# Second attention: values of four heads per group, a ring of eight heads' probabilities, value projections two slots later

## The chip, the cores and the metric

The kernel runs on one core of a Trainium2 chip. The metric is the device time of one execution in microseconds; lower is better. Most executions of a kernel agree within 0.3%.

## What is computed

Two transformer blocks on eight images of 16x16 tokens with 192 channels, in float32. The first block attends inside 14x14 windows (12 heads of 16 channels), the second over the whole image of 256 tokens (12 heads of 48 channels). Both add decomposed relative positions (a term by row and one by column) to the scores. Each attention is followed by an MLP of four times the width. The change is in the second block's attention:

```
xn = layernorm(x) * ln1_scale + ln1_offset          # per image: 256 tokens x 192
q = xn @ wq + bq;  k = xn @ wk + bk;  v = xn @ wv + bv   # 12 heads x 48
logits = q k^T / sqrt(48) + bias_h(q) + bias_w(q)   # per head: 256 x 256
attn = softmax(logits)
out = (attn @ v) @ wo + bo
x = x + out;  x = x + mlp(x)
```

## The kernel before

The program is written by hand for each engine's queue, with semaphores between them. It goes through four stages, each over the eight images: attention 0, MLP 0, attention 1, MLP 1 (classes `Attention0`, `Mlp`, `Attention1`; the base class `Attention` holds the common steps). All of x stays in the on-chip memory, as do the weights.

An image of attention 1 has 12 **slots**, one for each head (`run`, `step`; `pe_slot`, `act_slot` and `dve_slot` say what each engine does in slot u). The heads are software-pipelined: in slot u TensorE computes the scores of head u + 3 (L1239, two matmuls of 256 columns, 80 rows deep: 48 channels and 32 rows that carry the positions), then transposes the probabilities of head u into a PSUM bank (L1246, four transposes). ScalarE takes the exponentials of head u + 2 (L663), VectorE normalizes head u + 1 (L671, L674) and takes the maximum of head u + 3 (L653). The transposed probabilities are copied from PSUM into `PT1` (L693), by VectorE for every fourth head and by ScalarE for the others; `PT1` holds four heads, and the copy for head u waits until the values that read that place are done (`pt_free`).

The values of heads 2q and 2q + 1 are computed when both are copied: `pv_after` names the slot after which group q is complete, and `VALUES_BEHIND = 1` puts its matmuls (L1266, four of 256 columns: two key halves by two heads, each head on 64 columns of the array) into the next slot. So values stand in slots 2, 4, 6, 8, 10, and for the last pair in slot 0 of the next image. They fill 256 of the 512 columns of `O_BANK`; ScalarE copies them to `AO1` (L1274, `act_ao`) before the next pair may be written. In slot 1 the output projection follows (L1285, `pe_back`), in the same bank.

The next image's front is spread over the same slots (`pe_fronts`, `act_fronts`, `dve_fronts`). In slot 2 its normalized rows are transposed (L705) and scaled into `xnT`, a rounded `xnH`, and the low part of their difference (L1310, VectorE). Slots 3 to 5 compute its q and k (L1318, six matmuls for each half) from these, with evictions by ScalarE and VectorE; the first waits for the low part. At the end of slot 5 come 64 small matmuls for the position terms (L1378). In slot 6 ScalarE (L1397) and VectorE (L1405) copy these to `rel_dense`. Then SyncE and GpSimd each issue four transfers of 48 KB that spread them over the rows of the operand Q (L1436), behind the larger transfers of q and k (L1416, L1420). Slots 7 and 8 compute v for the two halves of the tokens (L1346, `pe_v`; 12 matmuls of 288 columns each). In slot 9 TensorE computes the first scores of the next image. They wait for all these transfers:

```
                if u == 0:
                    eng.wait_ge(self.scat, n.at(64, 64))
                    eng.wait_ge(self.relscat, n.at(64, 64))
                    eng.wait_ge(self.relscat_w, n.at(64, 64))
```

The front of the first image runs ahead of the stage without slots, and the last image has no follower, so seven images carry a front in their slots.

Of the kernel before, what the change touches and what calls it, by code (L numbers as in the profile page):

```python
# [39 lines left out]
P = 128  # L40
# [84 lines left out]
def build(nc, a, out):  # L125
    with ExitStack() as ctx:
# [117 lines left out]
        area = sb("area", [P, 2 * NT * HEADS * 64 + (8 + NPAIR) * T])  # L244
# [3 lines left out]
        PT1 = area[:, 3072:3072 + 8 * T].rearrange("p (b k q) -> p b k q", b=4, k=2)  # L248
        AO1 = area[:, 3072 + 8 * T:3072 + (8 + NPAIR) * T].rearrange("p (q t) -> p q t", q=NPAIR)
# [360 lines left out]
        class Attention:  # L610
# [76 lines left out]
            def pt_out(self, eng, n, u, copy):  # L687

                eng.wait_ge(self.t_rdy, n.at(self.NU, u + 1))
                per, k = self.pt_free(u)  # L690
                if n.counts(per, k):
                    eng.wait_ge(self.pv, n.at(per, k))
                copy(*self.pt_views(u)).then_inc(self.pt[self.pt_engine(u)], 1)  # L693
# [186 lines left out]
        class Attention0(Attention):  # L880
# [339 lines left out]
        class Attention1(Attention):  # L1220
            G_USES = (10, 10)
            G_OUTS = (11, 11)
            V_SLOT = 7
# [26 lines left out]
            def pt_views(self, u):  # L1250
# [19 lines left out]
            def act_ao(self, eng, n, q):  # L1270
                eng.wait_ge(self.pv, n.at(NPAIR, q + 1))
# [4 lines left out]
            def dve_ao(self, eng, n, q):  # L1276
                pass

            def pe_back(self, eng, n):
                eng.wait_ge(self.ao[0], n.at(NPAIR, NPAIR))  # L1280
# [74 lines left out]
            def act_v(self, eng, n, t):  # L1355
                eng.wait_ge(self.g_rdy[0], n.at(10, 9 + t))
                if n.counts(NPAIR, -NPAIR):
                    eng.wait_ge(self.pv, n.at(NPAIR, -NPAIR))
                nc.scalar.copy(*self.v_views(n, t, 0)).then_inc(self.g_out[0], 1)

            def dve_v(self, eng, n, t):
                eng.wait_ge(self.g_rdy[1], n.at(10, 9 + t))
                if n.counts(NPAIR, -NPAIR):
                    eng.wait_ge(self.pv, n.at(NPAIR, -NPAIR))
# [100 lines left out]
            def setup(self):  # L1465
# [6 lines left out]
                                  5: each(self.pe_qk, (5,)) + [self.pe_rel], 7: each(self.pe_v, (0,)),  # L1472
                                  8: each(self.pe_v, (1,))}
                self.act_fronts = {2: [self.act_xn], 3: each(self.act_q, (0, 1, 2)), 4: each(self.act_q, (3, 4)),
                                   5: each(self.act_q, (5,)), 6: [self.act_rel], 7: each(self.act_v, (0,)),
                                   8: each(self.act_v, (1,))}
                self.dve_fronts = {0: [self.dve_stats], 1: [self.dve_xhat], 2: [self.dve_xn], 3: each(self.dve_k, (0, 1, 2)),
                                   4: each(self.dve_k, (3, 4)), 5: each(self.dve_k, (5,)), 6: [self.dve_rel],
                                   7: each(self.dve_v, (0,)), 8: each(self.dve_v, (1,))}
# [4 lines left out]
                        {2 * q + 1: [q] for q in range(NPAIR)})  # L1484
# [289 lines left out]
```

## Time and profile before

| | |
|---|---|
| runs, us | 877.87, 874.0, 875.62 (median 875.62) |
| the profiled execution | 876.63 us, span 874.8 us |
| mean granted clock of TensorE | 0.967 |
| busy share of the span: TensorE / VectorE / ScalarE / GpSimd | 90% / 59% / 50% / 15% |
| attention 1 in the span | about 433 to 795 us |
| its scores / transposes / values, busy us | 108.1 / 59.8 / 53.3 |
| chain that ended last, by engine | TensorE 78%, VectorE 12%, issue 3%, ScalarE 3%, DMA 2% |

The span runs from the first to the last instruction; the execution's time has a little around it. A row of a timeline gives the start, the length, engine, line, operation, output and inputs with their shape, the count of merged instructions, and in brackets the idle time just before with what ended it.
### The profile page before, as it was taken

How to read it: one execution, taken by the hardware profiler on the slowest of the kernel's cores; microseconds unless marked ns; L12 is line 12 of the kernel's file. 1: busy time of each engine (PE TensorE's matmuls, PEld its weight loads, DVE VectorE, ACT ScalarE, POOL GpSimd, SP SyncE). 2: the span in 40 equal slices, each digit the busy share in tenths (PEclk: the TensorE clock that was granted, in tenths of full speed). 3: DMA queues.
4: the chain of work that ended last, by engine and by line, in shares of the span. 5: the costliest groups of instructions: out<-in, count | busy, mean ns of one | idle time of the engine just before them, and what ended most of it. 6: DMA issues, size and time to landing. Idle time of an engine off the chain costs nothing.

```text
span 874.8 us, 18893 instructions
## 1 busy us (share of the span) xinstructions
PE 787.8 (90%) x6794; PEld 641.5 (73%) x6794; DVE 518.5 (59%) x1518; ACT 434.4 (50%) x1421; POOL 127.7 (15%) x243
## 2 busy tenths in 40 slices
PE   3788989898898977789979999999999999997998
PEld 2566656575675744789967788888888888876998
DVE  6156777757667676454426565666666666674442
ACT  2045565645656554444335455555555555554432
POOL 7200110101111010142320101010101010101111
PEclk9989999989999997899987999999999999999999
DMA  7362101010110100100040404040404040400001
GB/s 144 73 147 36 20 17 25 11 33 10 29 20 17 29 8 1 37 1 1 1 73 0 73 2 73 1 74 1 73 1 74 1 75 1 74 1 1 19 22 34
DMA packets 38092, 29.23 MB, mean 33 GB/s; under 512 B 11926, under 2 KB 36274, under 8 KB 38000
## 3 DMA queue, kind: packets, MB, share of 16 engines
q1 hardware_dynamic: 34974, 25.71, 16.2%
q0 software_dynamic: 2048, 1.89, 1.2%
q8 instruction: 55, 0.90, 0.5%
q10 hardware_dynamic: 978, 0.43, 0.3%
q14 instruction: 37, 0.30, 0.1%
HBM read 7.94 MB, written 1.57 MB: 11 GB/s over the span
## 4 chain that ended last, share of the span: by engine, by line
PE 78%; DVE 12%; issue 3%; ACT 3%; DMA 2%; ACTq 1%; POOL 1%; SPq 1%; DVEq 0%; POOLq 0%
PE bank L1239 10%; PE bank L1318 8%; PE bank L475 7%; PE bank L496 7%; PE bank L1266 5%; PE bank L1246 5%; PE bank L1115 5%; PE bank L946 4%; PE bank L922 4%; PE bank L1285 4%; PE bank L1047 3%; PE bank L1378 3%; DVE Pb L674 2%; PE bank L973 2%; PE bank L1012 2%
## 5 line engine op out<-in xcount | busy, mean ns | idle before, releaser
L663 ACT ACTIVATE Pb<-bank,nmax 128x256 f32<-128x256 f32 (+1 forms) x432 | 191.9, 452 | 88.1 <-DVE nmax L653 85.7
L653 DVE TENSOR_REDUCE nmax<-bank 128x2 f32<-128x392 f32 (+2 forms) x240 | 138.8, 579 | 44.7 <-PE bank L1239 32.9
L674 DVE TENSOR_SCALAR Pb<-Pb,rsum 128x196 f32<-128x196 f32 (+2 forms) x432 | 133.7, 347 | 8.7 <-DVE rsum L671 0.2
L693 ACT COPY area<-bank 98x392 f32<-98x392 f32 (+1 forms) x144 | 77.3, 538 | 86.6 <-PE bank L1246 75.0
L1239 PE MATMUL bank<-QK 80*128 80x256 f32 x384 | 108.1, 407 | 8.1 <-DMA QK<-rel_dense 6.7
L1239 PEld LDWEIGHTS bank<-QK 80*128 80x128 f32 x384 | 69.7, 199 | 28.7 <-issue 16.2
L663 ACT ACTIVATION_READ_ACCUMULATOR Pb<-bank,nmax 128x1 f32 x432 | 87.4, 202 | 0.0
L946 PE MATMUL bank<-ident,Pb 128*98 128x128 f32 x384 | 64.0, 291 | 19.2 <-DVE Pb L674 19.1
L485 ACT ACTIVATE area<-bank,fc1b 128x256 f32<-128x256 f32 x96 | 45.1, 473 | 66.9 <-PE bank L475 66.9
L946 PEld LDWEIGHTS bank<-ident,Pb 128*98 128x98 f32 x384 | 41.5, 133 | 33.5 <-DVE Pb L674 28.2
L496 PE MATMUL bank<-fc2w,area 128*128 128x192 f32 x384 | 64.7, 326 | 0.0
L693 DVE COPY area<-bank 60x128 f32<-60x128 f32 (+2 forms) x96 | 43.4, 452 | 35.1 <-PE bank L949 18.2
L475 PE MATMUL bank<-xnH,fc_high 96*128 96x256 f32 x192 | 57.3, 298 | 7.1 <-DVE xnT_low L463 3.8
L496 PEld LDWEIGHTS bank<-fc2w,area 128*128 128x128 f32 x384 | 62.1, 190 | 0.0
L1246 PE MATMUL bank<-ident,Pb 128*128 128x128 f32 x384 | 59.8, 279 | 1.3 <-DVE Pb L674 1.3
L1246 PEld LDWEIGHTS bank<-ident,Pb 128*128 128x128 f32 x384 | 49.0, 144 | 12.9 <-DVE Pb L674 2.9
L475 PE MATMUL bank<-xnH,fc1w_low 96*128 96x256 f32 x192 | 55.1, 287 | 0.0
L475 PE MATMUL bank<-xnT_low,fc_high 96*128 96x256 f32 x192 | 55.0, 286 | 0.0
L1266 PE MATMUL bank<-area 128*64 128x256 f32 x384 | 53.3, 399 | 1.3 <-DVE area L693 0.8
L1337 DVE TENSOR_SCALAR dense<-bank,kb 96x256 f32<-96x256 f32 x48 | 23.0, 480 | 50.9 <-PE bank L1318 50.1
L391 POOL TENSOR_SCALAR lnve<-lnag 128x2 f32<-128x2 f32 x32 | 7.7, 241 | 294.7 <-DVE lnag L383 292.7
L922 PE MATMUL bank<-QK 64*128 64x196 f32 x384 | 47.8, 369 | 2.1 <-ACT Pb L663 1.3
(139 smaller groups left out, 1516.5 us busy)
## 6 DMA issues: line engine op xcount, KB each, us to landing
QK<-dense SPq DMA_DIRECT2D x32, 288.0 KB, 6.4
QK<-dense SPq DMA_DIRECT2D x48, 64.0 KB, 2.4
QK<-dense SPq DMA_DIRECT2D x90, 28.0 KB
QK<-rel_dense SPq DMA_DIRECT2D x32, 48.0 KB, 3.4
QK<-rel_dense POOLq DMA_DIRECT2D x32, 48.0 KB, 3.1
out<-x_all SPq DMA_DIRECT2D x8, 192.0 KB, 2.0
x_all<-in_x SPq DMA_DIRECT2D x1, 1344.0 KB, 16.3
QK<-in_c_hot SPq DMA_DIRECT2D x2, 384.0 KB, 4.6
```

What stands on the lines that cost most here:

```text
L475: mm = nc.tensor.matmul(self.hbank[(n.parity * NM + m) % 4][:, 0:T], w[:, c, m * P:(m + 1) * P], x[:, c, :], start=(c == 0 and i == 0), st ...
L496: mm = nc.tensor.matmul(ybank[:, t * C:(t + 1) * C], hT[n.parity][:, m, t * P:(t + 1) * P], fc2w[self.l][:, m, :], start=(m == 0), stop=(m ...
L653: nc.vector.tensor_reduce(nmax[0:sc.shape[0], u % 3, 0:sc.shape[1]], sc, AX.X, ALU.max, negate=True).then_inc(self.m_rdy, 1)
L663: nc.scalar.activation(Pb[u % 3][0:rows, t, 0:cols], sc[:, t, :], ACT.Exp, bias=nmax[0:rows, u % 3, t:t + 1], accum_out=esum[0:rows, u % 3 ...
L674: nc.vector.tensor_scalar(Pb[u % 3][0:rows, t, 0:keep], Pb[u % 3][0:rows, t, 0:keep], rsum[0:rows, u % 3, t:t + 1], None, ALU.mult).then_i ...
L693: copy(*self.pt_views(u)).then_inc(self.pt[self.pt_engine(u)], 1)
L922: mm = nc.tensor.matmul(S_BANK[(u + j) % 3][:, t * N0:(t + 1) * N0], Q0[p][rows, i, t * P:(t + 1) * P], k, start=True, stop=True)
L946: mm = nc.tensor.transpose(ptb[0:HT0, kc * T + t * P:kc * T + (t + 1) * P], pb[:, t, kc * HT0:(kc + 1) * HT0], ident[:])
L1239: mm = nc.tensor.matmul(S_BANK[u % 3][:, t * T:(t + 1) * T], Q1[p][:, u, t * P:(t + 1) * P], K1[p][:, u, :], start=True, stop=True)
L1246: mm = nc.tensor.transpose(PT_BANK[u % 2][:, kc * T + t * P:kc * T + (t + 1) * P], Pb[u % 3][:, t, kc * P:(kc + 1) * P], ident[:])
L1266: mm = nc.tensor.matmul(O_BANK[64 * j:64 * j + 64, 0:T], V1[p][:, kc, 2 * q + j, :], PT1[:, (2 * q + j) % 4, kc, :], start=(kc == 0), stop ...
L1318: mm = nc.tensor.matmul(G_BANK[b][0:CH, 0:T], w[:, c, g * CH:(g + 1) * CH], x[:, c, :], start=(c == 0 and i == 0), stop=(c == 1 and i == 2))
```

## The change

The values are now computed for four heads at a time: groups r = 0, 1, 2, complete after slots 3, 7 and 11, so that they stand in slots 4, 8 and, for the last, slot 0 of the next image. Two pairs lie beside each other in the full 512 columns of `O_BANK`, and one copy of 512 columns evicts them. `PT1` holds eight heads in two halves of four that alternate from group to group, also across images (`ring`). All counts of the semaphores `pv` and `ao` go by three groups in place of six pairs. The value projections move from slots 7 and 8 to slots 9 and 10 on all three engines. What each matmul computes, and how many there are, stays.

```diff
@@
-        area = sb("area", [P, 2 * NT * HEADS * 64 + (8 + NPAIR) * T])
+        area = sb("area", [P, 2 * NT * HEADS * 64 + (16 + NPAIR) * T])
...
-        PT1 = area[:, 3072:3072 + 8 * T].rearrange("p (b k q) -> p b k q", b=4, k=2)
-        AO1 = area[:, 3072 + 8 * T:3072 + (8 + NPAIR) * T].rearrange("p (q t) -> p q t", q=NPAIR)
+        PT1 = area[:, 3072:3072 + 16 * T].rearrange("p (b k q) -> p b k q", b=8, k=2)
+        AO1 = area[:, 3072 + 16 * T:3072 + (16 + NPAIR) * T].rearrange("p (q t) -> p q t", q=NPAIR)
@@
-            V_SLOT = 7
+            V_SLOT = 9
@@
-            def pt_views(self, u):
-                return PT1[:, u % 4, :, :].rearrange("p k q -> p (k q)"), PT_BANK[u % 2][:, 0:2 * T]
+            def pt_views(self, n, u):
+                return PT1[:, self.ring(n, u), :, :].rearrange("p k q -> p (k q)"), PT_BANK[u % 2][:, 0:2 * T]
+
+            def ring(self, n, u):
+
+                return 4 * (n.at(3, u // 4) % 2) + u % 4
 
             def pt_free(self, u):
-                return NPAIR, u // 2 - 1
-
-            def pe_values(self, eng, n, q):
+                return 3, u // 4 - 1
+
+            def pe_values(self, eng, n, r):
                 p = n.parity
                 for e in range(2):
-                    eng.wait_ge(self.pt[e], n.at(self.pt_cum[e][-1], self.pt_cum[e][2 * q + 2]))
-                if q == 0 and n.counts(1, 0):
+                    eng.wait_ge(self.pt[e], n.at(self.pt_cum[e][-1], self.pt_cum[e][4 * r + 4]))
+                if r == 0 and n.counts(1, 0):
                     eng.wait_ge(self.done, n.at(1, 0))
-                if n.counts(NPAIR, q):
-                    eng.wait_ge(self.ao[0], n.at(NPAIR, q))
-                for kc in range(2):
-                    for j in range(2):
-                        mm = nc.tensor.matmul(O_BANK[64 * j:64 * j + 64, 0:T], V1[p][:, kc, 2 * q + j, :],
-                                              PT1[:, (2 * q + j) % 4, kc, :], start=(kc == 0), stop=(kc == 1))
+                if n.counts(3, r):
+                    eng.wait_ge(self.ao[0], n.at(3, r))
+                for pair in range(2):
+                    for kc in range(2):
+                        for j in range(2):
+                            h = 4 * r + 2 * pair + j
+                            mm = nc.tensor.matmul(O_BANK[64 * j:64 * j + 64, pair * T:(pair + 1) * T], V1[p][:, kc, h, :],
+                                                  PT1[:, self.ring(n, h), kc, :], start=(kc == 0), stop=(kc == 1))
                 mm.then_inc(self.pv, 1)
...
-                nc.scalar.copy(AO1[:, q, :], O_BANK[:, 0:T]).then_inc(self.ao[0], 1)
+                nc.scalar.copy(AO1[:, 2 * r:2 * r + 2, :], O_BANK[:, 0:2 * T].rearrange("p (q t) -> p q t", q=2))\
+                  .then_inc(self.ao[0], 1)
@@
-                                  5: each(self.pe_qk, (5,)) + [self.pe_rel], 7: each(self.pe_v, (0,)),
-                                  8: each(self.pe_v, (1,))}
+                                  5: each(self.pe_qk, (5,)) + [self.pe_rel], 9: each(self.pe_v, (0,)),
+                                  10: each(self.pe_v, (1,))}
...
@@
-                        {2 * q + 1: [q] for q in range(NPAIR)})
+                        {4 * r + 3: [r] for r in range(3)})
```

What TensorE has in its queue from slot 6 to slot 9 before (L1239 scores, L1246 transposes, L1266 values, L1346 value projections; `QK_0` and `QK_1` are the operands of this image and the next; where a line of dots stands, the other rows of the same projection are left out):

```order
L1239 MATMUL bank0<-QK_0 128x256 x2
L1246 MATMUL bank3<-ident,Pb0 128x128 x4
L1266 MATMUL bank5<-area 64x256 x4
L1239 MATMUL bank1<-QK_0 128x256 x2
L1246 MATMUL bank4<-ident,Pb1 128x128 x4
L1346 MATMUL bank6<-wv1_high,xnH 128x288
...
L1239 MATMUL bank2<-QK_0 128x256 x2
L1246 MATMUL bank3<-ident,Pb2 128x128 x4
L1266 MATMUL bank5<-area 64x256 x4
L1346 MATMUL bank6<-wv1_high,xnH 128x288
...
L1239 MATMUL bank0<-QK_1 128x256 x2
```

And the same place now, up to slot 10 (L1272 is the values' line, L1353 that of the value projections):

```order
L1239 MATMUL bank0<-QK_0 128x256 x2
L1246 MATMUL bank3<-ident,Pb0 128x128 x4
L1239 MATMUL bank1<-QK_0 128x256 x2
L1246 MATMUL bank4<-ident,Pb1 128x128 x4
L1239 MATMUL bank2<-QK_0 128x256 x2
L1246 MATMUL bank3<-ident,Pb2 128x128 x4
L1272 MATMUL bank5<-area 64x256 x8
L1239 MATMUL bank0<-QK_1 128x256 x2
L1246 MATMUL bank4<-ident,Pb0 128x128 x4
L1353 MATMUL bank6<-wv1_high,xnH 128x288
...
L1239 MATMUL bank1<-QK_1 128x256 x2
```

Both projections and the pair of slot 6 have left the place ahead of the first scores of `QK_1`; the group of slot 8 has doubled.

TensorE in slots 2 and 3 before, from the transposes of the normalized rows (L705) to the first product of q (L1318):

```order
L705 MATMUL bank6<-ident,xhat 96x128 x2
L705 MATMUL bank7<-ident,xhat 96x128 x2
L1266 MATMUL bank5<-area 64x256 x4
L1239 MATMUL bank0<-QK_1 128x256 x2
L1246 MATMUL bank4<-ident,Pb0 128x128 x4
L1318 MATMUL bank6<-xnH,wq1_high 96x256
```

and now:

```order
L705 MATMUL bank6<-ident,xhat 96x128 x2
L705 MATMUL bank7<-ident,xhat 96x128 x2
L1239 MATMUL bank0<-QK_1 128x256 x2
L1246 MATMUL bank4<-ident,Pb0 128x128 x4
L1325 MATMUL bank6<-xnH,wq1_high 96x256
```

The pair between the transposes and the q product has gone to slot 4.

ScalarE in slots 6 and 7 before (L693 copies probabilities, L1274 values, L1397 the position terms; L663 exponentials, L1359 v):

```order
L693 COPY area<-bank3 128x512
L1274 COPY area<-bank5 128x256
L1397 COPY rel_dense<-bank6 64x3x128
L1397 COPY rel_dense<-bank6 64x48x8
L663 ACTIVATE Pb0,esum<-bank0,nmax 128x256 x2
L1359 COPY area<-bank6 128x6x48
```

and now:

```order
L693 COPY area<-bank3 128x512
L1404 COPY rel_dense<-bank6 64x3x128
L1404 COPY rel_dense<-bank6 64x48x8
L663 ACTIVATE Pb0,esum<-bank0,nmax 128x256 x2
L663 ACTIVATE Pb1,esum<-bank1,nmax 128x256 x2
```

The copy of values no longer stands between the copy of probabilities and those of the position terms.

## Rows read from the trace of the kernel before

**Rows 1.** One steady image: from:to, length, PE PEld DVE ACT POOL busy, PEclk, DMA share, GB/s.

```profile
543.50:586.65 43.15, 42.73 (x398) 35.60 (x396) 27.45 (x73) 24.37 (x79) 4.16 (x7) 1.00 0.22 38
```

**Rows 2.** TensorE's timeline, that image and the next: start, length, instruction, idle before.

```profile
576.35 1.13 PE L1239 MATMUL bank<-QK 80*128 80x256 f32 x4
...
580.27 0.40 PE L1346 MATMUL bank<-wv_high,xnH 96*128 96x288 f32 x1
...
581.97 1.03 PE L1239 MATMUL bank<-QK 80*128 80x256 f32 x4
...
584.38 0.40 PE L1346 MATMUL bank<-wv_high,xnH 96*128 96x288 f32 x1
...
586.68 1.10 PE L1239 MATMUL bank<-QK 80*128 80x256 f32 x4 [0.45 <-DMA QK<-rel_dense]
587.62 0.60 PE L1246 MATMUL bank<-ident,Pb 128*128 128x128 f32 x4
588.06 1.03 PE L1239 MATMUL bank<-QK 80*128 80x256 f32 x4
588.92 0.60 PE L1246 MATMUL bank<-ident,Pb 128*128 128x128 f32 x4
589.46 1.08 PE L1266 MATMUL bank<-area 128*64 128x256 f32 x8
590.47 1.13 PE L1239 MATMUL bank<-QK 80*128 80x256 f32 x4
591.44 0.60 PE L1246 MATMUL bank<-ident,Pb 128*128 128x128 f32 x4
```

**Rows 3.** The same timeline, cut off inside one group of values.

```profile
589.46 0.44 PE L1266 MATMUL bank<-area 128*64 128x256 f32 x2
```

**Rows 4.** TensorE's timeline at the same place one image later.

```profile
630.09 1.10 PE L1239 MATMUL bank<-QK 80*128 80x256 f32 x4 [0.64 <-ACT Pb L663]
```

**Rows 5.** ScalarE's timeline in slot 6 of that image.

```profile
577.96 0.58 ACT L693 COPY area<-bank 128x512 f32<-128x512 f32 x1 [3.74 <-PE bank L1246]
...
579.25 0.97 ACT L1397 COPY rel_dense<-bank 64x384 f32<-64x384 f32 x2
```

**Rows 6.** VectorE's timeline in slots 6 and 7 of that image.

```profile
578.13 1.13 DVE L1405 COPY rel_dense<-bank 64x384 f32<-64x384 f32 x2
...
579.49 0.61 DVE L674 TENSOR_SCALAR Pb<-Pb,rsum 128x256 f32<-128x256 f32 x2
580.47 0.69 DVE L693 COPY area<-bank 128x512 f32<-128x512 f32 x1 [0.37 <-PE bank L1246]
```

**Rows 7.** DMA issues of SyncE (SPq) and GpSimd there, from their timelines.

```profile
580.38 2.53 SPq L1436 DMA_DIRECT2D QK<-rel_dense  x4
...
580.84 2.11 POOL L1436 DMA_DIRECT2D QK<-rel_dense  x4 [27.12 <-ACT rel_dense L1397]
```

**Rows 8.** Busy time by stretch, columns as in rows 1: DMA share.

```profile
575.00:584.00 9.00, 9.00 (x108) 7.30 (x101) 5.58 (x11) 4.77 (x14) 3.12 (x5) 1.00 0.97 164
```

**Rows 9.** TensorE's timeline, first q/k product of the next image.

```profile
603.77 0.36 PE L1318 MATMUL bank<-xnH,wq_high 96*96 96x256 f32 x1
```

**Rows 10.** VectorE's timeline just ahead of it.

```profile
602.72 0.69 DVE L1310 TENSOR_TENSOR xnT_low<-xnT,xnH 96x512 fp32r<-96x512 f32 x1
```

**Rows 11.** TensorE's timeline, three long waits in this stage and the two MLPs.

```profile
365.58 0.38 PE L475 MATMUL bank<-xnH,fc_high 96*128 96x256 f32 x1 [1.88 <-DVE xnT_low L463]
...
455.64 7.17 PE L1239 MATMUL bank<-QK 80*128 80x256 f32 x16 [6.27 <-DMA QK<-rel_dense]
...
806.50 0.39 PE L475 MATMUL bank<-xnH,fc_high 96*128 96x256 f32 x1 [1.88 <-DVE xnT_low L463]
```

**Rows 12.** Busy time by stretch, columns as in rows 1: PEclk behind those waits.

```profile
366.00:369.00 3.00, 3.00 (x28) 3.00 (x27) 1.63 (x5) 1.73 (x4) 1.89 (x3) 1.00 0.01 3
453.40:470.40 17.00, 14.76 (x44) 11.48 (x46) 8.85 (x26) 7.57 (x25) 1.03 (x2) 0.50 0.02 3
808.40:811.70 3.30, 3.30 (x18) 3.30 (x17) 1.34 (x2) 1.23 (x3) 1.13 (x2) 0.50 0.00 0
```

More of the change, by code:

```diff
@@ L692, in pt_out @@
                     eng.wait_ge(self.pv, n.at(per, k))
-                copy(*self.pt_views(u)).then_inc(self.pt[self.pt_engine(u)], 1)
+                copy(*self.pt_views(n, u)).then_inc(self.pt[self.pt_engine(u)], 1)
             def g_free(self, eng, n, b, outs_before):
@@ L1248, in emit_probsT, with pt_views @@
                 return mm
[L1250 to L1251 removed]
+            def pt_views(self, n, u):
+                return PT1[:, self.ring(n, u), :, :].rearrange("p k q -> p (k q)"), PT_BANK[u % 2][:, 0:2 * T]
+            def ring(self, n, u):
+                return 4 * (n.at(3, u // 4) % 2) + u % 4
             def pt_free(self, u):
[L1254 to L1256 removed]
+                return 3, u // 4 - 1
@@ L1268, in pe_values, with act_ao @@
                 mm.then_inc(self.pv, 1)
-            def act_ao(self, eng, n, q):
-                eng.wait_ge(self.pv, n.at(NPAIR, q + 1))
+            def act_ao(self, eng, n, r):
+                eng.wait_ge(self.pv, n.at(3, r + 1))
                 if n.counts(1, 0):
                     eng.wait_ge(self.y, n.at(1, 0))
-                nc.scalar.copy(AO1[:, q, :], O_BANK[:, 0:T]).then_inc(self.ao[0], 1)
-            def dve_ao(self, eng, n, q):
+                nc.scalar.copy(AO1[:, 2 * r:2 * r + 2, :], O_BANK[:, 0:2 * T].rearrange("p (q t) -> p q t", q=2))\
+                  .then_inc(self.ao[0], 1)
@@ L1277, in dve_ao @@
+            def dve_ao(self, eng, n, r):
                 pass
             def pe_back(self, eng, n):
-                eng.wait_ge(self.ao[0], n.at(NPAIR, NPAIR))
+                eng.wait_ge(self.ao[0], n.at(3, 3))
                 if n.counts(1, 0):
@@ L1356, in act_v @@
                 eng.wait_ge(self.g_rdy[0], n.at(10, 9 + t))
-                if n.counts(NPAIR, -NPAIR):
-                    eng.wait_ge(self.pv, n.at(NPAIR, -NPAIR))
+                if n.counts(3, -3):
+                    eng.wait_ge(self.pv, n.at(3, -3))
                 nc.scalar.copy(*self.v_views(n, t, 0)).then_inc(self.g_out[0], 1)
@@ L1362, in dve_v @@
                 eng.wait_ge(self.g_rdy[1], n.at(10, 9 + t))
-                if n.counts(NPAIR, -NPAIR):
-                    eng.wait_ge(self.pv, n.at(NPAIR, -NPAIR))
+                if n.counts(3, -3):
+                    eng.wait_ge(self.pv, n.at(3, -3))
                 nc.vector.tensor_copy(*self.v_views(n, t, 1)).then_inc(self.g_out[1], 1)
@@ L1471, in setup @@
                 self.pe_fronts = {2: [self.pe_transpose_x], 3: each(self.pe_qk, (0, 1, 2)), 4: each(self.pe_qk, (3, 4)),
-                                  5: each(self.pe_qk, (5,)) + [self.pe_rel], 7: each(self.pe_v, (0,)),
-                                  8: each(self.pe_v, (1,))}
+                                  5: each(self.pe_qk, (5,)) + [self.pe_rel], 9: each(self.pe_v, (0,)),
+                                  10: each(self.pe_v, (1,))}
                 self.act_fronts = {2: [self.act_xn], 3: each(self.act_q, (0, 1, 2)), 4: each(self.act_q, (3, 4)),
-                                   5: each(self.act_q, (5,)), 6: [self.act_rel], 7: each(self.act_v, (0,)),
-                                   8: each(self.act_v, (1,))}
+                                   5: each(self.act_q, (5,)), 6: [self.act_rel], 9: each(self.act_v, (0,)),
+                                   10: each(self.act_v, (1,))}
                 self.dve_fronts = {0: [self.dve_stats], 1: [self.dve_xhat], 2: [self.dve_xn], 3: each(self.dve_k, (0, 1, 2)),
                                    4: each(self.dve_k, (3, 4)), 5: each(self.dve_k, (5,)), 6: [self.dve_rel],
-                                   7: each(self.dve_v, (0,)), 8: each(self.dve_v, (1,))}
+                                   9: each(self.dve_v, (0,)), 10: each(self.dve_v, (1,))}
         a0 = Attention0(0, lambda n: (ld_x0 if n.index0() else ld_x, 16), xdone[0], L0_UNITS, {6 * q + 5: [q] for q in range(3)})
```

## The prediction

> **What bounds the kernel now.** I read the stretches first. Over one steady image of the second attention (543.5 to 586.65) TensorE is busy 42.73 of 43.15 us at full clock, VectorE 27.45, ScalarE 24.37 [rows 1]. So in this stage TensorE's queue is the time: what it gains or waits there, the kernel gains or waits, once for each of the seven images whose projections run beside the image before (the eighth has no follower). The other engines have slack, but three things that TensorE needs arrive just in time, and the change touches all three.
>
> The TensorE timeline of one image [rows 2] prices the pieces. Transposes of a head take 0.44 us (587.62 to 588.06), scores 0.86 (588.06 to 588.92). Values of a pair take 1.01 (589.46 to 590.47), and beside them the transposes ahead take 0.54 (588.92 to 589.46) and the scores behind 0.97 (590.47 to 591.44). So a slot without values costs 1.30, and a pair of values adds 1.01 + 0.10 + 0.11 = 1.22. One V projection is 1.70 (580.27 to 581.97). From the first scores behind the position products (slot 6, 576.35) to the next image's first scores (slot 9), TensorE has three slots, two pairs and two V's: 584.38 + 1.70 = 586.08, that is 9.73 us. It then waits for the DMA of the position rows until 586.68: 0.45 us by the row. The wait at that place in the next image is 0.64 [rows 4]; it is put down to ScalarE, but ScalarE's exponentials that this slot needs were issued slots before, so I read it as the same DMA. In the others the rows show less, or nothing. Hence these transfers land about 9.7 to 10.4 us after slot 6 begins, and 9.73 us of TensorE's own work just covers them. Mean length of the stretch: about 9.9.
>
> **The change part by part.**
>
> *Merged groups.* Two matmul records of values end 0.44 us after their start [rows 3], all eight of a pair after 1.08 [rows 2]: 0.213 for each further two, 0.85 for eight more. A group of four heads then adds 1.22 + 0.85 = 2.07 where two pairs added 2.44: 0.37 saved per merge, three per image, 8.9 us over eight images if TensorE never waits. ScalarE swaps six copies of 128x256 for three of 128x512; a copy of that size from a bank takes 0.58 [rows 5]. It is off the path: ScalarE has 18 us per image to spare [rows 1]. Eight heads of held probabilities remove no wait: no row shows TensorE or an evictor waiting for room in the ring, and the new ring is freed a group before it is needed.
>
> *The stretch from slot 6 to slot 9.* It loses both V's (3.40 us), which go behind the wait, into slots 9 and 10. The pair of slot 6 goes too, and slot 8 has a group of four. TensorE: slots 6 and 7 at 1.30 bring it to 578.95; scores of slot 8 end at 579.81; its transposes need probabilities that VectorE finishes at 579.49 + 0.61 = 580.10, behind the position copies [rows 6]; the group needs VectorE's copy of head 7 (0.69), which follows at once, to 580.79. The group takes 0.85 + 1.01 = 1.86: TensorE stands at slot 9 at 582.7, 6.35 us after slot 6 began, where it stood at 9.73. It now waits there for the DMA.
>
> When do the transfers land? ScalarE's position copies sat behind the pair's copy and ended at 579.25 + 0.97 = 580.22; now they follow the copy of head 6 (577.96 + 0.58) and end at about 579.4, 0.8 earlier [rows 5]. VectorE's end at 579.26 anyway [rows 6]. SyncE and GpSimd issue on those [rows 7], so both start 0.8 us sooner. Bounds: all of the 0.8 arrives (landing 8.9 to 9.6 after slot 6), or nothing does, because the DMA engines are at 0.97 of their time from 575 to 584 with the q and k rows ahead [rows 8] (9.7 to 10.4). I take half, 9.5, as that row shows the engines full when the transfers are issued. Wait: 9.5 - 6.35 = 3.1 us (2.5 to 4.1). The stretch goes from 9.9 to 9.5.
>
> The Trainium skill, DMA: Bandwidth & Descriptors, section "Issuing engines are not separate DMA queues", says that transfers started by different engines end up on the same 16 DMA engines and interleave. By that rule alone the earlier issue would bring nothing and the wait would be about 3.5 to 4; by the issue times alone about 2.7. Rows 8 agree with the rule, but no run here shows the shift itself.
>
> *The rest of the image.* Slots 9 to 5 gain the two V's, 3.40 us. They had four pairs (slots 10, 0, 2, 4), now two groups of four (0, 4): 4.88 to 4.14, less 0.74.
>
> *Slot 2 without values.* TensorE transposes the next image's normalized rows in slot 2 and begins its q/k products in slot 3, at 603.77 [rows 9]. Without the pair it gets there 1.22 earlier, 602.55. But those products need the low part, which VectorE starts at 602.72 and ends at 603.41 [rows 10]; the chain hangs on the same transposes and does not move. New wait: 0.9 us (0.5 to 0.9, as the pair's switching cost is counted or not).
>
> Sum per image: -0.4 (slot 6 to 9) + 3.40 - 0.74 + 0.9 = +3.15. Seven images: +22. The last image, where TensorE waits for the others anyway, may save 0.4. The profiled execution took 876.6 us (span 874.8 and 1.8 around it), 1.0 above the median of the three runs; on the median 875.6 the sum gives 897.
>
> *TensorE's clock.* After the wait of 6.27 us at the start of this stage [rows 11] the granted clock was 0.50, which is 1.2 of 2.4 GHz, for 17 us [rows 12]. After a wait of 1.88 at 806.50 it was 0.50 for 3.3 us; after one of 1.88 at 365.58 it stayed at 1.00. A wait of 3.1 lies between these, seven times over. A stretch of 3.3 us at the lower level does half its work, 1.6 us lost; the scores and transposes stretch of 17 us lost over 7. I take a fall in half the images at 2.5 us each: 7 x 0.5 x 2.5 = 9 us. Ends: nothing, and 7 x 3.3 = 23.
>
> Forecast: 875.6 + 21.5 + 9 = **906 us**.
>
> The Trainium skill, TensorE: Matmul & The Clock Gate, section "HAM oscillation — how this bites in real kernels", describes a loop that waits for a DMA in each pass, loses the clock in each wait and starts each pass cold. By that rule the fall would come in every image, 23 us with two low stretches each, and 920 us; without it 897. Rows 11 and 12 show falls after some waits and not after one, so I stand between.
>
> **The rivals.**
>
> *The clock holds.* The waits come as worked out, the clock stays up: 897 us (890 to 903 with the landing at 8.9 or 10.3). For it: the wait of 1.88 without a fall. Chance 0.30.
>
> *The clock falls long.* In each image the low stretch lasts as the 17 us one did, since what follows the wait is scores and transposes again: 7 x 6 us more, about 940. Against it: V projections, dense work, now follow at once. Chance 0.10.
>
> *No wait at slot 9.* The position rows land by 582.7 because their issue, moved up, gets them in between the q and k rows. Then slot 6 to 9 takes 6.35 and the image is 3.55 shorter there and 3.55 longer in the rest: no change, 872 to 877. It decides at a landing 3 us earlier than any row shows; against it stand the full engines [rows 8]. Chance 0.08.
>
> *Faster.* The evictors, relieved of waits for values in slots 2 and 6, deliver both what slot 3 and what slot 9 needs before TensorE comes: the merges' 8.9 and the old waits' 1.4 are all that is left, 865. It needs the low part 0.9 us sooner as well as the landing. Rows 10 speak against it: that chain starts from TensorE's own transposes. Chance 0.06. That the change doesn't do what it says I see no room for: the order of rows shows the groups and the V's moved.
>
> **How the numbers follow.** Forecast 0.46, clock holds 0.30, long falls 0.10, no wait 0.08, faster 0.06. The range from 888 to 925 takes in the forecast's and the first rival's bounds and leaves out long falls, no change and faster. Slower by over 0.5% (4.4 us, about what a measurement can tell): 0.86; within it 0.08; faster 0.06.
>
> **What would show it.** In the changed profile: in each of seven images a wait of 2.5 to 4 us before the next image's first scores, put down to the DMA of the position rows; about 0.9 us before the first q/k product, put down to the low part; groups of 16 records, 1.86 us apart from the next scores; position transfers issued 3.2 us after slot 6 begins instead of 4.0; low granted clock behind some of the waits. Wrong if the wait at slot 9 is under 1 us, or if the period from slot 9 to slot 9 (43.4 us now, from 586.68 to 630.09) grows by less than 1.

## The result and the profile after

The changed kernel takes 917.03 us (median of four runs, 913.03 to 918.71) against 876.75 (874.0 to 881.08) of the kernel before on the same chip: ratio 1.0459, 95% interval 1.0424 to 1.0495, 40 us slower. The forecast was 906, in a range from 888 to 925. The profiled execution took 918.54 us, with a span of 916.7 and a mean granted clock of 0.94 (before 0.967). Of all executions behind the numbers below one, of the groups of four with the cut output projection, ran slow throughout (1120.59 us at a mean granted clock of 0.638); it stands in no median and no ratio here.

Lines of code have shifted by six or seven: values are L1272 now, their copy L1280, output projection L1292, low part L1317, q and k products L1325, value projections L1353, position products L1385, position copies L1404 and L1412, position transfers L1443.

The page of the profile after (parts 1, 2 and 4: busy time, the granted clock by slice, the chain that ended last):

```profile
PE 803.5 (88%) x6794; PEld 662.6 (72%) x6794; DVE 523.0 (57%) x1518; ACT 433.1 (47%) x1397; POOL 128.1 (14%) x243
...
PEclk9989999999999976899969899979799999999999
...
PE 71%; DVE 13%; issue 5%; DMA 4%; ACT 4%; SPq 2%; ACTq 1%; POOL 1%; DVEq 0%; POOLq 0%
```

TensorE's share of the span fell from 90 to 88% although it is busy for longer, and in the middle of the span the clock has dents that come back at an even distance.

To see where the 40 us lie, take the second attention alone, from the second of the two value projections that run ahead of its slots to the first product of the MLP behind it. The view by stretch, after and then before (columns as in rows 1):

```profile
452.19:841.52 389.33, 350.32 (x2962) 297.40 (x2963) 215.74 (x561) 187.11 (x571) 36.84 (x58) 0.93 0.19 32
```

```profile
446.70:799.63 352.93, 338.71 (x2962) 279.23 (x2963) 212.88 (x561) 189.19 (x595) 36.82 (x58) 0.97 0.21 36
```

The stage is 36.4 us longer: TensorE is idle for 39.0 us in place of 14.2 (+24.8), and busy for 350.3 in place of 338.7 (+11.6) with the same matmuls. The view of waits over that stretch (who waits for whom: total, times, longest), after:

```profile
PE bank L1239 <- DMA QK<-rel_dense: 26.5, 8, 5.6
PE bank L1325 <- DVE xnT_low L1317: 4.5, 7, 0.7
PE bank L1246 <- DVE Pb L674: 2.3, 2, 1.2
PE bank L1385 <- issue: 2.0, 2, 1.1
```

and before:

```profile
PE bank L1239 <- DMA QK<-rel_dense: 6.7, 2, 6.3
PE bank L1378 <- issue: 1.3, 1, 1.3
PE bank L1246 <- DVE Pb L674: 1.3, 3, 0.7
```

Scores wait 19.8 us more for the position rows, and the q products 4.5 us for the low part, for which they never waited: together 24.3 of the 24.8. The eight waits of the first row are the one at the start of the stage (5.59, before 6.27 [rows 11]) and one in each image with a follower: 2.35, 3.23, 3.44, 3.64, 3.13, 2.17 and 2.93 us. TensorE's timeline of the third, from slot 6 on:

```profile
590.03 1.13 PE L1239 MATMUL bank<-QK 80*128 80x256 f32 x4
...
594.61 1.95 PE L1272 MATMUL bank<-area 128*64 128x256 f32 x16
600.00 1.99 PE L1239 MATMUL bank<-QK 80*128 80x256 f32 x4 [3.44 <-DMA QK<-rel_dense]
601.79 1.06 PE L1246 MATMUL bank<-ident,Pb 128*128 128x128 f32 x4
602.50 0.59 PE L1353 MATMUL bank<-wv_high,xnH 96*128 96x288 f32 x1
602.89 0.44 PE L1353 MATMUL bank<-wv_low,xnH 96*128 96x288 f32 x1
603.13 0.44 PE L1353 MATMUL bank<-wv_high,xnT_low 96*128 96x288 f32 x1
```

The last two of these records, before:

```profile
580.51 0.30 PE L1346 MATMUL bank<-wv_low,xnH 96*128 96x288 f32 x1
580.64 0.30 PE L1346 MATMUL bank<-wv_high,xnT_low 96*128 96x288 f32 x1
```

The rows answer to [rows 2]. Two value projections and one pair no longer stand ahead of the first scores, TensorE is there 3.2 us sooner (at 600.00 - 3.44 = 596.56, that is 6.53 us after slot 6 began, where it was 9.73) and waits. What follows is slow: four records of scores take 1.99 us where they took 1.10, transposes 1.06 where 0.60, and the records of the projection follow each other at 0.24 us in place of 0.13. The view by stretch behind that wait, and behind the next (columns as in rows 1; the granted clock stands behind POOL):

```profile
600.00:610.00 10.00, 10.00 (x36) 9.07 (x37) 2.53 (x6) 2.73 (x8) 0.00 (x0) 0.50 0.01 2
610.50:620.00 9.50, 9.50 (x64) 8.05 (x63) 6.48 (x20) 5.08 (x19) 1.04 (x2) 1.00 0.00 0
651.50:661.50 10.00, 10.00 (x37) 9.08 (x37) 2.53 (x6) 2.96 (x9) 0.00 (x0) 0.50 0.01 2
```

At 0.50 (1.2 of 2.4 GHz) 36 matmul records run in 10 us; at 1.00, 64 in 9.5. Counted in this view in steps of half a microsecond, the clock is low behind all seven waits, for 6.8, 3.4, 10.2, 10.2, 3.4, 3.4 and 3.4 us: 40.9 us, of which I count half, some 20.4, as lost. Before, there was one stretch of 3.4 us beside the one at the start (17.07 in both). The difference, 18.7, is more than the 11.6 by which TensorE's busy time grew. I put the 7.1 between them down to the merged groups; measured apart, at full clock, they save 0.87 in each of the eight images, 7.0 (last experiment).

### The profile page after: what moved, and what is told of

It reads as the page before. It is cut to its first block, busy times and chain, and to the rows that moved or that the text cites. A ratio compares the mean times of both kernels' runs of the same rounds, so it can differ in the third digit from the quotient of the medians.

```text
span 916.7 us, 18820 instructions
## 1 busy us (share of the span) xinstructions
PE 803.5 (88%) x6794; PEld 662.6 (72%) x6794; DVE 523.0 (57%) x1518; ACT 433.1 (47%) x1397; POOL 128.1 (14%) x243
## 4 chain that ended last, share of the span: by engine, by line
PE 71%; DVE 13%; issue 5%; DMA 4%; ACT 4%; SPq 2%; ACTq 1%; POOL 1%; DVEq 0%; POOLq 0%
PE bank L1239 8%; PE bank L1325 8%; PE bank L475 7%; PE bank L496 7%; PE bank L1115 4%; PE bank L1246 4%; DMA QK<-rel_dense 4%; PE bank L922 3%; PE bank L1292 3%; PE bank L1353 3%; PE bank L946 3%; PE bank L1272 3%; PE bank L1047 3%; DVE Pb L674 3%; PE bank L1385 3%
## 5 line engine op out<-in xcount | busy, mean ns | idle before, releaser
L663 ACT ACTIVATE Pb<-bank,nmax 128x256 f32<-128x256 f32 (+1 forms) x432 | 192.0, 451 | 100.2 <-DVE nmax L653 98.0
L674 DVE TENSOR_SCALAR Pb<-Pb,rsum 128x196 f32<-128x196 f32 (+2 forms) x432 | 138.6, 358 | 8.7 <-DVE rsum L671 0.2
L1239 PE MATMUL bank<-QK 80*128 80x256 f32 x384 | 112.1, 420 | 26.5 <-DMA QK<-rel_dense 26.5
L693 ACT COPY area<-bank 98x392 f32<-98x392 f32 (+1 forms) x144 | 77.2, 537 | 111.3 <-PE bank L1246 99.6
L1239 PEld LDWEIGHTS bank<-QK 80*128 80x128 f32 x384 | 72.7, 207 | 41.1 <-issue 16.8
L663 ACT ACTIVATION_READ_ACCUMULATOR Pb<-bank,nmax 128x1 f32 x432 | 86.9, 201 | 0.0
L1246 PE MATMUL bank<-ident,Pb 128*128 128x128 f32 x384 | 64.0, 293 | 2.9 <-DVE Pb L674 2.3
L475 PE MATMUL bank<-xnH,fc_high 96*128 96x256 f32 x192 | 59.4, 309 | 7.1 <-DVE xnT_low L463 3.8
L1246 PEld LDWEIGHTS bank<-ident,Pb 128*128 128x128 f32 x384 | 51.7, 152 | 18.0 <-DVE Pb L674 7.1
L475 PE MATMUL bank<-xnT_low,fc_high 96*128 96x256 f32 x192 | 56.9, 296 | 0.0
L693 DVE COPY area<-bank 60x128 f32<-60x128 f32 (+2 forms) x96 | 43.3, 451 | 19.2 <-PE bank L949 17.3
L1272 PE MATMUL bank<-area 128*64 128x256 f32 x384 | 46.7, 385 | 1.6 <-issue 0.8
```

The lines of the kernel that those rows point to most:

```text
L475: mm = nc.tensor.matmul(self.hbank[(n.parity * NM + m) % 4][:, 0:T], w[:, c, m * P:(m + 1) * P], x[:, c, :], start=(c == 0 and i == 0), st ...
L663: nc.scalar.activation(Pb[u % 3][0:rows, t, 0:cols], sc[:, t, :], ACT.Exp, bias=nmax[0:rows, u % 3, t:t + 1], accum_out=esum[0:rows, u % 3 ...
L674: nc.vector.tensor_scalar(Pb[u % 3][0:rows, t, 0:keep], Pb[u % 3][0:rows, t, 0:keep], rsum[0:rows, u % 3, t:t + 1], None, ALU.mult).then_i ...
L693: copy(*self.pt_views(n, u)).then_inc(self.pt[self.pt_engine(u)], 1)
L1239: mm = nc.tensor.matmul(S_BANK[u % 3][:, t * T:(t + 1) * T], Q1[p][:, u, t * P:(t + 1) * P], K1[p][:, u, :], start=True, stop=True)
L1246: mm = nc.tensor.transpose(PT_BANK[u % 2][:, kc * T + t * P:kc * T + (t + 1) * P], Pb[u % 3][:, t, kc * P:(kc + 1) * P], ident[:])
```

## The experiments

All ratios are to the kernel before, run on the same chip beside each; the changed kernel is 1.0459. First the two halves of the change were run apart.

**Groups of four alone: the changed kernel with the value projections back in slots 7 and 8.**

```diff
-            V_SLOT = 9
+            V_SLOT = 7
-                                  5: each(self.pe_qk, (5,)) + [self.pe_rel], 9: each(self.pe_v, (0,)),
-                                  10: each(self.pe_v, (1,))}
+                                  5: each(self.pe_qk, (5,)) + [self.pe_rel], 7: each(self.pe_v, (0,)),
+                                  8: each(self.pe_v, (1,))}
```

(and likewise for ScalarE and VectorE)

> The changed kernel with the value projections back in slots 7 and 8; groups of four and the ring of eight stay. Theory (the moved projections leave TensorE waiting for the DMA of the position rows in slot 9): that wait falls from about 3 us to 0.2 to 0.9 in each of seven images, no low clock behind it; the wait of 0.65 us for the low part in slot 3 stays. Sum against the kernel before: -8.9 (merged groups) + 4.5 (slot 3) + about 2, so 871 to 878 us. Rival (the group of four itself, late and long, is the cost): waits of 2 us and more stay somewhere in slots 4, 8 or 0, and the time stays above 900.

Measured: 879.67 us, ratio 1.005 (1.0032 to 1.0067), 1.7 us above the expected range. Its waits over the stage, and the stage by stretch:

```profile
PE bank L1239 <- DMA QK<-rel_dense: 5.8, 2, 5.4
PE bank L1325 <- DVE xnT_low L1317: 3.9, 6, 0.6
PE bank L1246 <- DVE Pb L674: 2.3, 2, 1.2
PE bank L1353 <- ACT rel_dense L1404: 1.4, 6, 0.2
```

```profile
449.92:803.71 353.79, 335.42 (x2962) 283.39 (x2962) 211.40 (x561) 186.36 (x571) 36.81 (x58) 0.97 0.21 35
```

The long waits at slot 9 are gone, and with them the low clock between the images' slots, except for 6.8 us from 708.83 on, behind an idle time of 1.38 us before the position products. Those for the low part stay, so they belong to the groups and not to the projections' move, and 0.24 before the first value projection is new. In the trace the stage is 0.9 us longer than before: TensorE's idle time grew by 4.2 us and the low clock by 3.4 (1.7 lost), so its work is some 5.0 shorter, less than the 7.0 of the last experiment. The rest of the 4.4 us by the ratio lies outside the stage or between executions; the runs do not place it.

**The projections' move alone: the kernel before, with them in slots 9 and 10.**

```diff
-            V_SLOT = 7
+            V_SLOT = 9
-                                  5: each(self.pe_qk, (5,)) + [self.pe_rel], 7: each(self.pe_v, (0,)),
-                                  8: each(self.pe_v, (1,))}
+                                  5: each(self.pe_qk, (5,)) + [self.pe_rel], 9: each(self.pe_v, (0,)),
+                                  10: each(self.pe_v, (1,))}
```

> The kernel before (pairs, ring of four) with the value projections in slots 9 and 10. Theory: TensorE reaches slot 9 6.3 us after slot 6 and waits 3.3 to 3.9 us for a landing at about 10, in seven images, with the clock falling behind the waits as in the changed kernel; no wait in slot 3. 877 + 7 x 3.4 + about 18 = 914 to 924 us, that is as slow as the changed kernel. Rival (groups are the cost): 872 to 882.

Measured: 908.33 us, ratio 1.0373 (1.0306 to 1.044), 6 us under the expected range. Waits at slot 9 of 3.21, 2.99, 3.43, 2.78, 3.22, 3.45 and 3.49 us, none before the q products; low clock behind six of the seven. So of the change's 40 us some 33 come with the move of the projections alone, and some 4 with the groups alone.

**Filler in the wait: the changed kernel with 18 matmuls of 288 columns, whose results nobody reads, ahead of the next image's first scores.**

```diff
+                if u == 0 and n.counts(1, 0):
+                    self.g_free(eng, n, 0, 9)
+                    for _ in range(18):
+                        nc.tensor.matmul(G_BANK[0][:, 0:HEADS * D1 // 2], xnH[:, 0, 0:P],
+                                         wv1s[1][:, 0, 0:HEADS * D1 // 2], start=True, stop=True)
```

> The changed kernel with 18 more matmuls (2.4 us of dense work, into a bank that is free there, results overwritten) ahead of the first scores of each of the seven following images, where TensorE would else sit idle. Theory (the idle time costs twice, once as a wait and again by the clock that falls behind it, about 20 us in the seven images): the clock stays at 1.00 in most images, the first scores start at the same time after slot 6 as without the matmuls, and the time is 896 to 904 us. Rival (the clock falls for another reason, the DMA traffic or the scores and transposes behind it): the low stretches stay and the time is 915 to 925.

Measured: 898.29 us, ratio 1.026 (1.0221 to 1.0299). TensorE's timeline (scores stand in L1244 here) with the stretch behind a wait that remained, and the same stretch of another image:

```profile
589.00 2.66 PE L1237 MATMUL bank<-wv_high,xnH 96*128 96x288 f32 x18
592.98 1.63 PE L1244 MATMUL bank<-QK 80*128 80x256 f32 x4 [1.31 <-DMA QK<-rel_dense]
```

```profile
593.00:596.40 3.40, 3.40 (x13) 3.00 (x14) 0.69 (x1) 0.58 (x1) 0.00 (x0) 0.56 0.01 2
640.40:650.00 9.60, 9.60 (x66) 8.52 (x68) 5.81 (x16) 4.75 (x17) 0.00 (x0) 1.00 0.00 0
```

The filler does nothing useful and the landing is no earlier (9.4 to 10.5 us after slot 6 begins in the six images that still wait), yet the kernel is some 18 us faster: 40.3 less the 22.8 by the ratio. In five of seven images no low clock follows; it does behind the two longest waits left (1.31 and 1.36). The stage by stretch:

```profile
447.13:824.37 377.24, 355.67 (x3089) 302.78 (x3089) 215.16 (x561) 186.89 (x571) 36.80 (x58) 0.96 0.20 33
```

It is 12.1 us shorter than in the changed kernel. The clock is low in it for 30.7 us in place of 58.0 (the 17.1 at the start in both), and half of that difference is 13.7. The other 5 us by which the two profiled executions differ lie ahead of the stage, which begins at 447.13 here and at 452.19 there. So TensorE's idle time does cost twice. Of the 36.4 us in the stage 18.7 are the clock by the trace of the changed kernel; the filler, with four low stretches left beside the one at the start, gives back 12 of them.

**What sets the landing: ScalarE's position copies one slot later, so that the transfers are issued 0.9 us later.**

```diff
-                                   5: each(self.act_q, (5,)), 6: [self.act_rel], 9: each(self.act_v, (0,)),
+                                   5: each(self.act_q, (5,)), 7: [self.act_rel], 9: each(self.act_v, (0,)),
```

> The changed kernel with ScalarE's copies of the position terms moved from slot 6 to slot 7, behind its two exponentials there (some 0.9 us), so that the position transfers are issued about 4.1 us after slot 6 begins, as in the kernel before (4.0), in place of 3.2; nothing else moves. Theory (the landing is set by how long the DMA engines take for the q and k rows and these, not by the issue): landing stays near 10.0 us after slot 6, waits at slot 9 of 3.0 to 3.5, 914 to 920. Rival (landing follows the issue): landing near 10.8, waits 0.8 us longer in seven images, about 923 (921 to 926).

Measured: 913.2 us, ratio 1.0434 (1.0395 to 1.0474), no slower than the changed kernel. SyncE's timeline of the changed kernel in the image above, then SyncE's and TensorE's of this one at the same place:

```profile
587.10 1.25 SPq L1423 DMA_DIRECT2D QK<-dense  x2
588.47 2.30 SPq L1427 DMA_DIRECT2D QK<-dense  x2
593.25 2.54 SPq L1443 DMA_DIRECT2D QK<-rel_dense  x4
```

```profile
587.36 2.53 SPq L1443 DMA_DIRECT2D QK<-rel_dense  x4
```

```profile
583.24 1.13 PE L1239 MATMUL bank<-QK 80*128 80x256 f32 x4
...
593.02 1.63 PE L1239 MATMUL bank<-QK 80*128 80x256 f32 x4 [3.25 <-DMA QK<-rel_dense]
```

Issued 3.22 us after slot 6 begins, they land 9.97 after it; issued 4.12 after, they land 9.78 after. Over the seven images the waits have a mean of 3.19 us in place of 2.98 (TensorE comes to slot 9 at 6.53 us in both). Most of that comes from the first image (3.40 and 2.35); the other six differ by 0.07 in the mean. So of 0.9 us of issue 0.2 or less reach the landing: the rows wait for the DMA engines, which show 1.07 of their time busy from 591 to 597 in the changed kernel (more than 1, since the view counts a transfer whole where it starts):

```profile
591.00:597.00 6.00, 5.37 (x37) 3.84 (x35) 5.63 (x11) 4.31 (x13) 3.13 (x5) 1.00 1.07 155
```

**The counterpart: the q and k rows leave sooner.** In the changed kernel their four transfers are cut in two, and the first halves are issued when their projections are done; the position rows are issued as before.

```diff
-                    eng.wait_ge(self.g_out[0], n.at(11, 7))
-                    land(eng, "sp")
-                    for j in range(2):
-                        eng.dma_start(Q1[p][0:D1, j:HEADS:2, :], self.qd[D1 * j:D1 * (j + 1), :, :]).then_inc(self.scat, 16)
...
+                    for g in (0, 3):
+                        for b, (dst, src) in enumerate(((Q1[p], self.qd), (K1[p], self.kd))):
+                            eng.wait_ge(self.g_out[b], n.at(11, 4 + g))
+                            land(eng, "sp")
+                            for j in range(2):
+                                eng.dma_start(dst[0:D1, 2 * g + j:2 * g + 6:2, :],
+                                              src[D1 * j:D1 * (j + 1), g:g + 3, :]).then_inc(self.scat, 16)
```

> The changed kernel with the q and k transfers cut in two: the rows of the first six heads leave once their projections are done, three heads' products earlier, the rest as before. Same bytes, eight issues instead of four. Theory (the position rows land late because the DMA engines are still full of q and k rows when they are issued): they land about 7 us after slot 6 begins instead of 10, the wait in slot 9 falls from 3 us to under 1, the clock holds, and the time is 878 to 890 us. Rival (the landing is set by the position transfers' own issue and latency): the wait stays at 2.5 us or more and the time above 908.

Measured: 885.88 us, ratio 1.0137 (1.0092 to 1.0182). TensorE's and SyncE's timelines:

```profile
623.12 1.13 PE L1239 MATMUL bank<-QK 80*128 80x256 f32 x4
...
631.09 1.10 PE L1239 MATMUL bank<-QK 80*128 80x256 f32 x4 [1.44 <-DMA QK<-rel_dense]
```

```profile
626.34 2.52 SPq L1442 DMA_DIRECT2D QK<-rel_dense  x4
```

The position rows are issued at the same point, 3.22 us after slot 6, and land 7.97 after it in place of 9.97, since less lies ahead of them. The waits shrink to 1.44 to 1.51 us in six images (expected under 1), and behind none of these does the clock fall. In the first image TensorE doesn't wait: it runs at 0.50 itself ahead of slot 9, for 10.2 us behind an idle time of 0.99 at the end of slot 5. Two microseconds of landing per image gave back 28 us of the 40, some 5 of them at the start of the stage, where the wait went from 5.59 to 2.27 and the low clock behind it from 17.1 to 13.7.

**The wait for the low part.** From the groups of four with the projections in slots 7 and 8, the output projection is cut in two: one tile of tokens stays in slot 1, the other goes to slot 2 behind the transposes of the normalized rows, where a pair of values stood before. (VectorE's step that takes up the finished projection moves to slot 2 with it.)

```diff
+            BACK = {1: (0,), 2: (1,)}
-                if u == self.VALUES_BEHIND and has_prev:
-                    self.pe_back(eng, n.prev())
+                if u in self.BACK and has_prev:
+                    self.pe_back(eng, n.prev(), self.BACK[u])
```

> The groups of four with the value projections back in slots 7 and 8, and the output projection cut in two: its first half stays in slot 1, its second goes to slot 2, behind the transposes of the normalized rows, where the pair of values stood before. Theory (the merge saves TensorE's work, and slot 3 gives it back because nothing stands between those transposes and the q products): the waits of 0.64 to 0.65 us before the first q product go in seven images, 4.5 us, from 879.7 to about 875 (873 to 877). Rival (the merge saves no work of TensorE, the waits are only where a lag of the evictors shows): the time appears as a wait elsewhere and the run stays at 878 to 881.

> A second look at the groups of four in slots 7 and 8 with the cut output projection, for its trace. Theory: no wait for the low part in the steady images, waits at slot 9 of 0.2 to 1.2 us since TensorE now comes there sooner, 870 to 876. Rival: waits in slot 3 as in the run without the cut.

Measured: 872.55 us (median of eleven runs), ratio 0.9955 (0.993 to 0.998); one more run took 870.2, and its trace is read here. Its waits over the stage (L1243 scores, L1250 transposes, L1358 value projections):

```profile
PE bank L1243 <- DMA QK<-rel_dense: 6.2, 2, 5.8
PE bank L1250 <- DVE Pb L675: 2.3, 2, 1.2
PE bank L1358 <- ACT rel_dense L1409: 1.7, 7, 0.2
```

The row for the low part is gone, and at slot 9 two short waits remain (0.46 and 0.21). Covered at both ends, the groups beat the pairs by 4 us. The same cut in the changed kernel, with the projections in slots 9 and 10:

> The changed kernel (value projections in slots 9 and 10) with the output projection cut in two, the second half behind the transposes of the normalized rows in slot 2. Theory (the waits add up): the waits for the low part in slot 3 go, 4.5 us, and those at slot 9 stay as they were, 2.2 to 3.6 us with a low clock behind them: 912 to 914. Rival (the waits hide one another: less time in slot 3 only lets TensorE come sooner to slot 9): 916 to 919.

Measured: 906.2 us, ratio 1.0354 (1.0299 to 1.0409), 9 us under the changed kernel with some 6 us of uncertainty. That is below both expected ranges, a miss. In its trace the waits for the low part are gone but for one of 0.6, and those at slot 9 are longer (23.8 in sum in place of 20.9), as the rival said: of the 4.5 us some 2.9 come back there. The low clock behind them lasts 34.1 us in place of 40.9 and at the start of the stage 13.7 in place of 17.1, which is 5 us less lost; why, no run shows.

**Both covers: that kernel with the q and k transfers cut in two as well, and the kernel before with that cut alone.**

> The same with the q and k transfers cut in two, so that the first halves of the rows leave earlier. Theory: the rest of the waits at slot 9 (0.2 to 0.7 in three images, 1.4 in sum) go, the wait at the start of the stage shrinks from 5.6 to about 2.3 us, as it did with the same cut in the changed kernel, and the low stretch behind it from 17 to 13.7 us: 1.4 + 3.3 + 1.7 = 6.4 off 875, about 869 (866 to 872), faster than the kernel before by 0.3 to 1.1%. Rival (the landing matters only where the cover is gone): 874 to 877.

> The kernel before with the q and k transfers cut in two and nothing else. Theory: its own waits at slot 9 (0.45 and 0.64 in two images) go, and the wait at the start of the stage shrinks by 3.3 us with 1.7 for the clock behind it: about 869.5 (867 to 872). Rival (eight issues in place of four on SyncE's queue delay the position rows as much as the first halves gain): 874 to 877.

Measured: 862.97 us, ratio 0.9846 (0.9803 to 0.9889), and 866.95, ratio 0.9893 (0.9853 to 0.9934). Both gain some 9.5 us from the cut, more than the 6 expected. Each has a wait of 2.3 us at the start of the stage and 10.2 us of low clock behind it, where before had 6.27 and 17.07. One steady image of each, by stretch (columns as in rows 1), the groups of four first:

```profile
593.40:635.30 41.90, 41.66 (x399) 35.86 (x398) 27.30 (x72) 23.50 (x72) 4.16 (x7) 1.00 0.17 39
```

```profile
594.23:636.76 42.53, 42.53 (x398) 35.66 (x397) 27.07 (x72) 23.87 (x75) 4.16 (x7) 1.00 0.16 39
```

Here the merge stands by itself, at full clock: TensorE is busy for 41.66 us per image with groups of four and for 42.53 with pairs. Of the 0.87 saved, 0.24 goes to the wait before the first value projection. The groups with both covers have the lowest median of this study, 1.5% under the kernel before; the 4 us between the two kernels here are within the uncertainty of their ratios, and that the groups are the faster rests on the traces.

## Why the prediction was right, and where it was off

**The mechanism, each step.** That TensorE would reach slot 9 some 3.4 us sooner and wait there for the position rows, seven times over, is what the trace shows (3.2 us sooner): arrival 6.53 us after slot 6 begins (forecast 6.35), landing 9.97 in that image and 6.53 + 2.98 = 9.5 in the mean (forecast 9.5, bounds 8.9 to 10.4), waits of 2.17 to 3.64, mean 2.98 (forecast 3.1, 2.5 to 4.1). SyncE issued the position rows 3.22 us after slot 6 began (forecast 3.2).

**How much of the earlier issue arrives.** I took half of the 0.8 us, between nothing and all. The run with the issue put back by 0.9 us shows that 0.2 of it or less arrives: the landing is the time the full DMA engines need, and it moves when the q and k rows leave sooner. The end that rests on rows 8 was the nearer one. The Trainium skill, DMA: Bandwidth & Descriptors, section "Issuing engines are not separate DMA queues", says that transfers run on the same 16 DMA engines and interleave whichever engine started them. The two runs agree with it: 0.2 us of landing for 0.9 of issue, but 2.0 for q and k rows that leave sooner. The mean landing is the forecast's 9.5 all the same, since the landings of before lay under the 9.7 to 10.4 that I read from two images with a wait [rows 2, 4].

**The low part.** Forecast 0.9 us (0.5 to 0.9), measured 0.60 to 0.65 in all seven images. The price without the pair's switching cost was right: 1.01 us off 603.77 is 602.76, that is 0.65 before 603.41.

**The merges.** Forecast 0.37 us each, 1.11 per image. In steady images without other waits it is 0.87 for three, 0.29 each.

**The sum without the clock.** Forecast +21.5 us. In the trace the stage grew by 36.4, of which 18.7 is the clock: 17.7. Its parts: waits at slot 9 and at the start +19.8, the low part +4.5, the merges -7.1. Of the 3.8 us that the forecast had too much, 1.8 are the low part (6.3 forecast, 4.5 measured) and 0.7 the shorter wait at the start of the stage; the rest the runs do not place.

**The clock: the mis-sized step.** I took "a fall in half the images at 2.5 us each", 9 us. It fell in every image, and cost some 20.4 us in the seven, 2.9 each, against 1.7 between the slots of before: 18.7 in place of 9. That 906 is no further from 917 is in part luck: the 9.7 that the clock's term had too little stand against the 3.8 that the rest of the sum had too much, so the stage alone would have come out at 912 (875.6 + 36.4). The last 5 us lie outside the stage or in the medians. What I set against a fall, one wait of 1.88 us after which the clock held [rows 11, 12], weighed too much: over the four kernels with the projections in slots 9 and 10 and nothing in the wait (the changed one, pairs, late copies, cut projection) the clock fell at 26 of 28 waits of 2.2 to 3.8 us. The two that held were 2.99 us (pairs) and 3.40 (late copies), so the length of the wait alone does not decide it. The Trainium skill's rule of TensorE: Matmul & The Clock Gate, section "HAM oscillation — how this bites in real kernels", a loop that loses its clock at each pass's wait, said this; the traces agree, with 26 of 28, and in the changed kernel with seven of seven. The prediction's 920 by that rule was nearer than its 906.

**The rivals.** "The clock holds" (897) is near the run with filler (898.3), in which it fell behind two of the waits all the same, and does not describe the change. Its lower end of 890 doesn't follow from its own landing of 8.9: 897 less seven times 0.6 is 893. "Falls long" (940) rested on low stretches like the 17 us at the start; the longest between the slots of the changed kernel is 10.2, twice, although value projections, dense work, follow at once: they too ran at half clock until then. "No wait at slot 9" and "faster" needed an earlier landing. That is what the cut transfers bring. With them, the low part's wait covered and the projections back in slots 7 and 8, the groups run in 863 us; that this is near the rival's 865 is chance, since some 7 us of it were gained at the start of the stage, which the rival did not count.

**What stays open.** The medians differ by 40.3 us, the stage in the two traces by 36.4. In the profiled run after, the stage began 5.5 us later (452.19 against 446.70), ahead of all that the change reorders; in the other kernels' traces that start lies between 445.8 and 452.2 without regard to what they change. Whether the timed runs share this, their times alone do not tell. Why a low stretch lasts 3.4 us once and 10.2 another time, with the same work behind it, no run settles.

## What to carry to other kernels

Work that stands between the issue of a transfer and its use is cover: before moving it, measure the time from the issue's place to the landing and count what TensorE has left in between. A wait opened on the engine that bounds the kernel is to be priced with the clock behind it; here the 21 us waited at slot 9 brought another 20 by half of the low time behind them. Merging groups to save switches also takes cover away at the places where the old groups stood; the saving showed only when both places were filled again.

## What the runs showed of the hardware that was not expected

The position rows' landing moved by only 0.2 us in the mean with an issue 0.9 us later (by 0.07 without the first image), but by 2.0 us when other transfers left sooner.

Low clock lasts through dense work: in two images of the changed kernel both value projections behind the wait ran at 0.50 up to the last few records, 10.2 us in all, and in others the same work was back at 1.00 after 3.4.

A longer wait can leave the clock up and a shorter one lose it: it held after 2.99 us (pairs, with a value projection behind it) and fell after 1.31 us behind the filler. The stretch behind the former, by the view by stretch (granted clock 1.00, where the same columns read 0.50 above):

```profile
543.20:553.20 10.00, 10.00 (x67) 8.44 (x69) 5.01 (x14) 4.33 (x14) 0.00 (x0) 1.00 0.01 2
```

The clock also fell behind short idle times that are no wait for the position rows: at the position products TensorE stands still in some images for 0.70 to 1.38 us, waiting for nothing that the profile shows. The clock fell behind four of eleven such times in the traces (0.99, 1.22, 1.33 and 1.38) and held behind seven (0.70 to 1.07). The shortest of the four had the longest low stretch behind it, 10.2 us, in the run with the early q and k rows:

```profile
486.63 0.25 PE L1385 MATMUL bank<-dense,relw_w 96*32 96x48 f32 x1 [0.99 <-issue]
```

```profile
487.50:497.50 10.00, 10.00 (x36) 7.32 (x37) 6.84 (x15) 4.05 (x12) 3.11 (x5) 0.50 0.21 51
```
